# Summing the exponentials of two groups on VectorE before the product with ones, in unit 3 of an attention layer

## What is computed

```python
attn = jnp.einsum('bhqd,bhkd->bhqk', Q, K) * scale
attn = jnp.where(causal, attn, -jnp.inf)
probs = jax.nn.softmax(attn, axis=-1)
y = jnp.einsum('bhqk,bhkd->bhqd', probs, V)
y = y.transpose(0, 2, 1, 3).reshape(Bx, Sx, Dm)
return y @ W_O.T
```

## Time and profile before

| | us |
|---|---|
| median of 3 runs | 2440.8 (2438.86 to 2441.42) |
| profiled execution | 2442.9 |
| its span, first to last instruction | 2441.2 |
| PE busy | 2295.5 (94%) |
| DVE busy | 1453.3 (60%) |
| ACT busy | 1072.6 (44%) |
| POOL busy | 861.4 (35%) |
| product with ones (den_ps), 3072 instructions | 319.0 |
| product with v (y_ps), 3072 instructions | 327.3 |

### The profile page before, as it was taken

One profiled execution on the slowest core, in us unless ns is written; L12 is line 12 of the kernel. 1 busy time (PEld: TensorE's weight loads), 2 busy tenths in 40 slices (PEclk: granted clock), 3 DMA queues, 4 the chain that ended last, 5 costly groups with the idle time before them and its releaser, 6 DMA issues.

```text
span 2441.2 us, 42231 instructions
## 1 busy us (share of the span) xinstructions
PE 2295.5 (94%) x14012; PEld 1467.3 (60%) x14013; DVE 1453.3 (60%) x3928; ACT 1072.6 (44%) x2186; POOL 861.4 (35%) x1519
## 2 busy tenths in 40 slices
PE   1999999999999999999999999999999999959998
PEld 1755575547654675457554765477546755437886
DVE  2577366644775367736674576537763667466776
ACT  2245424462345324542446234632454244625665
POOL 2232324232423333332423242334233242235666
PEclk9999999999999999999999999999999999969999
DMA  8533145313533154314432353225322444344554
GB/s 297 148 96 104 61 113 150 111 66 91 152 102 103 45 159 109 97 64 120 147 105 70 87 158 102 96 55 172 103 80 70 128 119 122 102 148 134 162 163 130
DMA packets 131537, 283.11 MB, mean 116 GB/s; under 512 B 33110, under 2 KB 42334, under 8 KB 128928
## 3 DMA queue, kind: packets, MB, share of 16 engines
q1 hardware_dynamic: 102352, 212.79, 29.3%
q0 software_dynamic: 27472, 67.49, 9.5%
q10 hardware_dynamic: 1536, 0.53, 0.1%
HBM read 135.10 MB, written 46.48 MB: 74 GB/s over the span
## 4 chain that ended last, share of the span: by engine, by line
PE 78%; DVE 7%; SPq 5%; DMA 3%; ACT 2%; issue 2%; POOL 1%; ACTq 0%; POOLq 0%; DVEq 0%
PE y_ps L1349 12%; PE proj L1260 10%; PE den_ps L1349 10%; PE score L1329 10%; PE maxp L1317 8%; PE proj L1372 5%; SPq L514 5%; PE proj L1273 4%; PE maxp L1514 4%; PE score L1514 4%; PE proj L1317 3%; PE maxp L1329 2%; DVE tile_max L1008 2%; PE score L1372 2%; ACT probs L872 2%
## 5 line engine op out<-in xcount | busy, mean ns | idle before, releaser
L872 ACT ACTIVATE probs<-score 128x512 f32<-128x512 f32 (+3 forms) x1216 | 563.5, 493 | 541.5 <-PE score L1329 519.8
L712 POOL TENSOR_SCALAR_AFFINE_SELECT probs<-probs 128x256 f32<-128x256 f32 x512 | 217.0, 428 | 707.1 <-ACT probs L872 704.2
L1013 DVE CUSTOM_DVE_ANT_0 maxp<-maxp,mask_qk 128x384 f32<-128x384 f32 (+3 forms) x696 | 323.1, 505 | 215.2 <-PE maxp L1317 209.4
L1329 PE MATMUL score<-q_stack,k_stack 97*128 97x512 f32 (+2 forms) x1216 | 425.9, 373 | 23.5 <-ACT probs L872 21.4
L1260 PE MATMUL proj<-xt,w_qk 128*128 128x512 f32 x1284 | 363.3, 399 | 54.3 <-DMA w_qk<-w_qk_parts 53.4
L1317 PE MATMUL maxp<-k_stack,q_stack 96*128 96x512 f32 (+2 forms) x1024 | 329.3, 365 | 11.4 <-DVE tile_max L1008 4.4
L1349 PE MATMUL y_ps<-probs,v 128*32 128x512 f32 (+3 forms) x3072 | 327.3, 498 | 12.1 <-DVE rows L1038 12.0
L1349 PE MATMUL den_ps<-probs,ones_f 128*32 128x512 f32 (+3 forms) x3072 | 319.0, 486 | 0.0
L1329 PEld LDWEIGHTS score<-q_stack,k_stack 97*128 97x128 f32 x1216 | 224.4, 189 | 139.5 <-ACT probs L872 92.3
L1260 PEld LDWEIGHTS proj<-xt,w_qk 128*128 128x128 f32 x1284 | 237.9, 190 | 110.3 <-DMA w_qk<-w_qk_parts 51.2
L1317 PEld LDWEIGHTS maxp<-k_stack,q_stack 96*128 96x128 f32 x1024 | 180.3, 188 | 137.3 <-DVE tile_max L1013 44.6
(11 more groups left out here) (159 smaller groups left out, 3157.2 us busy)
## 6 DMA issues: line engine op xcount, KB each, us to landing
w_qk<-w_qk_parts SPq DMA_DIRECT2D x64, 512.0 KB, 4.1
q_stack<-w_vo_parts SPq DMA_DIRECT2D x16, 2048.0 KB, 8.1
q_stack<-parts SPq DMA_DIRECT2D x512, 64.0 KB
k_stack<-parts SPq DMA_DIRECT2D x512, 64.0 KB
rows<-dispatched SPq DMA_DIRECT2D x75, 257.0 KB, 2.9
xt_raw<-x_t SPq DMA_DIRECT2D x32, 512.0 KB, 3.8
q_stack<-parts POOLq DMA_DIRECT2D x256, 64.0 KB, 2.3
k_stack<-parts POOLq DMA_DIRECT2D x256, 64.0 KB, 2.3
```

The source lines that it names most:

```text
L712: nc.gpsimd.affine_select(out=block, in_=block, compare_op=ALU.is_ge, fill=0.0, base=0, pattern=[[0, 2], [1, P]], channel_multiplier=-1)\
L872: nc.scalar.activation(probs[:, 4 * (n % PROBS) + h, c:BANK], score_bank(u, 4 * j + h)[:, c:BANK], ACT.Exp, scale=SCALE).then_inc(exp_done ...
L1013: top = nc.vector.tensor_tensor_reduce(out=tile, in0=tile, in1=mask_qk[:, BANK - cols:BANK], scale=1.0, scalar=-3.0e38, op0=ALU.add, op1=A ...
L1329: nc.tensor.matmul(score_bank(u, i)[:, c0:BANK], k_st[u % SETS][0:3 * DH + 1, h, kb * P:(kb + 1) * P], q_st[u % SETS][0:3 * DH + 1, h, t * ...
```

## The change

In unit 3 of every pass, groups 4 and 5, and groups 6 and 7, form a pair (`PAIRS`). VectorE adds the two groups' exponentials, all four heads in one instruction of 128 x 4 x 512, into a new tensor `late_sum` (`add_pair`). The product with ones is left out for the first group of a pair, and for the second it reads `late_sum`. So there are two groups of products with ones where there were four. The product with v stays for each group, and now signals `probs_used` for these. ScalarE waits for the pair's sum before it overwrites one of its groups (groups 7 to 10). The first add stands in VectorE's order at group 6 between `copy_y` and `turn_sums`, the second at group 8 ahead of the first residual. There is one `late_sum`, so the second add also waits for the first pair's product.

`late_sum` lies in the same memory as `w_qk`. The loads of unit 0's weights are therefore moved from `send(b, 3)` to behind `load_x(2)`, with a wait for the second pair's product.

```diff
--- before.py
+++ after.py
@@ -181,6 +181,8 @@
         with nc.sbuf_tensor("last_weight", [P, 2 * KT * D], F32), nc.sbuf_tensor("bias", [P, EXPERTS * D], F32) as bias:
             pass
         probs = sb("probs", [P, 4 * PROBS, BANK])
+        with nc.sbuf_tensor("late_sum", [P, 4, BANK], F32) as late_sum:
+            pass
         w_qk = sb("w_qk", [P, 2, 2, KT, P], F32R)
         parts = sb("parts", [P, 2, 2, BANK], F32R)
         rows = sb("rows", [P, ROWT, ROW])
@@ -289,6 +291,9 @@
         exp_done = signal("exp_done", UNITS * STILES)
         probs_masked = signal("probs_masked", UNITS * 2 * DIAGONAL)
         probs_used = signal("probs_used", UNITS * GROUPS)
+        PAIRS = ((4, 5), (6, 7))
+        pair_added = signal("pair_added", len(PAIRS))
+        pair_used = signal("pair_used", len(PAIRS))
         y_copied = signal("y_copied", UNITS * HALVES)
         sums_copied = signal("sums_copied", UNITS * HALVES)
         recip_done = signal("recip_done", UNITS * HALVES * 2)
@@ -498,6 +503,12 @@
             t, kb = SCORE_GROUPS[j]
             return kb * P >= t * BANK
 
+        assert all(SCORE_GROUPS[j][0] == 1 and SCORE_GROUPS[j][1] < HALF0 for pair in PAIRS for j in pair)
+
+        def pair_of(u, j):
+
+            return next((p for p, pair in enumerate(PAIRS) if u == UNITS - 1 and j in pair), None)
+
         def masks_up_to(u, j):
 
             return 2 * (DIAGONAL * u + sum(map(diagonal, range(j + 1))))
@@ -534,8 +545,8 @@
                 for o in (Q, K):
                     for t in range(HALVES):
                         send_tile(sp, b, u, o, t, range(SP_BLOCKS), sp_in)
-                    if not (u == UNITS - 1 and b == BATCHES - 1):
-                        load_w((u + 1) % UNITS, o)
+                    if u < UNITS - 1:
+                        load_w(u + 1, o)
 
             def load_expert(e):
                 if e >= RAWS:
@@ -591,6 +602,10 @@
                 for tb in range(2, ROWT):
                     wait_job(sp, b, proj_free, ("o", tb - 2))
                     load_x(tb)
+                    if tb == 2 and not last:
+                        sp.wait_ge(pair_used.sem, pair_used.at(b, len(PAIRS)))
+                        load_w(0, Q)
+                        load_w(0, K)
                 if not last:
                     send(b, 0)
 
@@ -866,6 +881,9 @@
                             split_high(k, xt_in[k % 2].at(b, 16 * (k // 2 + 1)))
                         n = GROUPS * u + j
                         weighed(act, b, max(n - PROBS + 1, 0))
+                        over = pair_of(u, j - PROBS)
+                        if over is not None:
+                            act.wait_ge(pair_added.sem, pair_added.at(b, over + 1))
                         for h in range(4):
                             c = column(kb, t)
                             act.wait_ge(score_full.sem, score_full.at(b, 4 * n + h + 1))
@@ -1038,6 +1056,14 @@
                     nc.vector.tensor_copy(y_of(n), y_ps[:, :].rearrange("p (t q) -> p t q", q=P))\
                         .then_inc(y_copied.sem, 1)
 
+                def add_pair(u, p):
+
+                    first, second = [probs[:, 4 * ((GROUPS * u + j) % PROBS):4 * ((GROUPS * u + j) % PROBS) + 4, :]
+                                     for j in PAIRS[p]]
+                    scored(dve, b, GROUPS * u + PAIRS[p][1] + 1)
+                    dve.wait_ge(pair_used.sem, pair_used.at(b, p))
+                    nc.vector.tensor_tensor(late_sum[:, :, :], first, second, ALU.add).then_inc(pair_added.sem, 1)
+
                 squares = lambda a: a.rearrange("p (c r) -> p c r", r=DH)
 
                 def turn_sums(n):
@@ -1095,9 +1121,13 @@
                             turn_sums(2 * u - 1)
                         if j == HALF0 + LAG:
                             copy_y(2 * u)
+                            if u == UNITS - 1:
+                                add_pair(u, 0)
                             turn_sums(2 * u)
                             if u == UNITS - 1:
                                 divide(2 * u)
+                        if u == UNITS - 1 and j == PAIRS[1][1] + 1:
+                            add_pair(u, 1)
                         due = maxima(u, j)
                         for i in due[0:2]:
                             reduce_tile(u + 1, i)
@@ -1341,16 +1371,25 @@
                         pe.wait_ge(exp_done.sem, exp_done.at(b, 4 * (n + 1)))
                         if diagonal(j):
                             pe.wait_ge(probs_masked.sem, probs_masked.at(b, masks_up_to(u, j)))
-                    if kb == 0:
+                    pair = pair_of(u, j)
+                    if sums_too and pair is not None:
+                        if j == PAIRS[pair][0]:
+                            return
+                        pe.wait_ge(pair_added.sem, pair_added.at(b, pair + 1))
+                    first = (j if pair is None or not sums_too else PAIRS[pair][0]) in (0, HALF0)
+                    if first:
                         free = sums_copied if sums_too else y_copied
                         pe.wait_ge(free.sem, free.at(b, half))
                     for h in range(4):
                         head = 4 * u + h
                         mm = nc.tensor.matmul((den_ps if sums_too else y_ps)[DH * h:DH * (h + 1), c:BANK],
                                               ones_f[:, :] if sums_too else v[:, kb, head * DH:(head + 1) * DH],
-                                              probs[:, 4 * (n % PROBS) + h, c:BANK], start=kb == 0, stop=last,
+                                              late_sum[:, h, :] if sums_too and pair is not None else
+                                              probs[:, 4 * (n % PROBS) + h, c:BANK], start=first, stop=last,
                                               tile_position=(0, DH * h), skip_group_check=True)
-                    if sums_too:
+                    if sums_too and pair is not None:
+                        mm.then_inc(pair_used.sem, 1)
+                    elif sums_too or pair is not None:
                         mm.then_inc(probs_used.sem, 1)
 
                 def transpose_max(u):
```

## The result

The changed kernel takes 2458.7 us (median of 4 runs, 2456.2 to 2462.2) where the kernel before took 2440.6 beside it: 1.0071 times as long, 95% interval 1.0056 to 1.0087. That is 18.1 us slower. The forecast was 2455.6.

What follows compares the result with a forecast made beforehand. TensorE, busy in 94% of the span, was taken to bound the kernel. Eight passes each 1.0 longer (-1.72 + 0.4 + 2.3) gave +8.0, the clock +6.8: 2440.8 + 14.8 = 2455.6 us, range 2443 to 2465.

Steps and rivals of the forecast that it cites:

- The gain: Unit 3, TensorE: two groups of sums removed at 0.86 each, 1.72 a pass, at most 13.8 us in eight passes.
- The first pair: Groups 4 and 5: TensorE stands 0.4 for the turned sums, and the product ends 0.46 earlier than before.
- The second pair: Groups 6 and 7: the add holds GpSimd's low part, TensorE stands 2.3 before output 0, pass 1.0 longer.
- The bound from the masks: GpSimd masks stood until VectorE's two-input instruction ended; so y's low part ends 1.15 behind the add, +1.0 a pass.
- rival B: The low part isn't held by the add; output 0 starts 0.55 earlier each pass, 2436.4 us; chance 0.13.
- The last pass: VectorE's splitting of expert weights stands between the adds; taken as the other passes, bounds 0 to +2.3.
- the add is always first: Unit 3: the second add starts ahead of GpSimd's low part, which also needs ScalarE's high part.
- The clock: TensorE's 2.3 us stall can bring 3.4 us at half speed, about 1.7; taken in four passes, +6.8, bounds 0 to +13.6.
- rival A: The forecast itself: low part held, clock falls in two to seven passes, 2452.2 to 2460.7 us; chance 0.42.
- A2: Low part held, clock falls in at most one pass: 2448.8 to 2450.5 us, down to 2443.2; chance 0.27.
- The sum: Whole kernel: +8.0 for the passes and +6.8 for the clock make +14.8, so 2455.6 us.
- The moved loads: Unit 0's weight loads in SyncE's queue: cost nothing, with over 20 us of cover; without it up to 6 us a pass.

Runs made afterwards that it cites:

- e8_early_high: Changed kernel with the order of e6_both, plus ScalarE making y tile 0's high part in the middle of group 7; 0.9937 of the kernel before, -15.4 us.
- e6_both: Changed kernel with the second add waiting for the low parts of y tiles 0 and 1, and the turning ahead of the first add; 0.9973 of the kernel before.
- e1_low_first: Changed kernel with VectorE's second add waiting until GpSimd has made the low parts of y tiles 0 and 1; 0.9986 of the kernel before, -3.4 us.
- e5_split: Changed kernel with the second add cut into four instructions of 128x512, one a head; 0.9986 of the kernel before, -3.4 us.
- e3_second_pair: Changed kernel with only groups 6 and 7 added on VectorE, groups 4 and 5 keeping their own products; 1.0103 of the kernel before, +25.2 us.
- e10_fill9: Changed kernel with nine throwaway matmuls on TensorE ahead of output 0's wait; 1.0027 of the kernel before, +6.6 us.
- e4_moved_loads: Changed kernel with no pairs or adds, only unit 0's weight loads moved; 0.9998 of the kernel before, -0.5 us.

## Why the prediction was right

**The gain** was taken as 2 x 0.86 = 1.72 a pass. e8_early_high, where nothing else arrives late in seven of the passes, gives 1.86 a pass there, 13.6 us in all eight unit 3s, and 15.4 us in all against the 13.8 that I took as the most; within its interval (11.0 to 19.6) that is the same.

**The first pair.** Forecast: a wait of about 0.4 for the turned sums, and the product done 0.46 earlier than before. Measured: the wait is 0.41 in seven passes (2.9 us in all), but the product behind it took 1.07 where 0.86 was put, so it was done 0.25 earlier. The eight instructions themselves are hardly slower. TensorE's timeline of before has, in the row from which the 0.86 was read:

```profile
531.21 1.07 PE L1349 MATMUL y_ps<-probs,v 128*32 128x512 f32 x8
532.09 1.04 PE L1349 MATMUL den_ps<-probs,ones_f 128*32 128x512 f32 x8
```

From first start to last end they took 1.04 there too, but the first 0.19 of it lay under the end of the product with v (532.28), and behind a wait that overlap is gone. Alone the pair gives 0.26 a pass. The step was right and the term 0.2 too good. e6_both removes the wait, and unit 3 is 0.62 a pass shorter than in e1_low_first, which is the 0.41 and the 0.21 together.

**The second pair.** The order was as forecast: group 7's exponentials, at once the add, and the low part inside it. From the end of the add to that of the low part I had 1.15, and it was 1.13; e1_low_first and e5_split, with the same work, show that the place of the add and the length of one instruction decide. The bound from the masks thus held for a subtraction with two operands too, as the Trainium skill ("SBUF — State Buffer", Who interferes with whom) has it, and rival B is out. Output 0 started 1.27 later than before in place of 1.0; the 0.2 of the first pair's product is most of the difference.

**The last pass** I had between 0 and +2.3, taken as +1.0. Its timeline:

```profile
2133.13 2.28 DVE L992 TENSOR_TENSOR weight<-w_raw,weight 128x2048 fp32r<-128x2048 f32 x1
...
2134.97 4.66 POOL L734 TENSOR_TENSOR parts<-rows,parts 128x512 fp32r<-128x512 f32 x2 [11.79 <-ACT parts L861]
...
2135.33 3.35 DVE L1065 TENSOR_TENSOR late_sum<-probs 128x2048 f32<-128x2048 f32 x1
...
2136.68 3.01 PE L1411 MATMUL proj<-q_stack,parts 128*128 128x512 f32 x12 [1.07 <-POOL parts L734]
```

Here the low part came while the expert's subtraction ran, ended 1.12 behind it at 2136.53, and VectorE's add, which was queued, stood until then: 3.35 in place of 2.29. GpSimd got in first, TensorE stood 1.07, and the pass lost 0.3 at most. So "the add is always first" was wrong for this pass, in which VectorE comes to the add only behind the expert's subtraction, and so was the fear that the add would slip in ahead of a low part that already waits; e5_split shows the latter in every pass.

**The clock.** Each stall of 2.36 could cost 1.7, in four of eight passes as I took it, from one row of before. It costs 1.6 (4.57 against 2.94), and it came in seven passes of one profile and four of the other, and in six of eight of e3_second_pair: 17 of 22 such stalls, where I had taken half. The four passes were a choice between none and eight and not worked out from anything, so this term was too small, and nothing in the rows of before could have sized it. So rival A stands, with the profile of the first result at its upper end, and A2 (no falls) is what e10_fill9 shows when the falls are taken away, +6.6 (4.1 to 9.3) to be compared with the forecast of +8; of the changed kernel itself no profile was without falls.

**The sum.** From the profile: seven passes with 1.27 + 1.6 and a last with 0.3 are 20.4 us in unit 3 (7 x 2.86 + 0.2 by the exponentials); the spans differ by 16.6 and the medians by 18.1. The rest, some 2 to 4 us the other way, lies in unit 0 and in the closing and opening between passes. The latter are 2.8 shorter in all than before, but in the variants, all of which have the same loads moved, they are anything from 2.6 shorter to 3.4 longer, so nothing follows from it for the change. My sum of 14.8 was put together from 8.0 of hold (measured 9.2) and 6.8 of clock (11.2 in one profile, less in the other). Both terms were too small, by 5.6 together, and that the forecast of 2455.6 came within 3.1 us of the measured 2458.7 is in part luck, since 2 to 4 us went the other way elsewhere. The mechanism is what the prediction had right.

**The moved loads** were put at nothing, and e4_moved_loads says the same.

## What to carry to other kernels

Before work is moved to an idle VectorE, look at what GpSimd does in the same microseconds, and at who waits for GpSimd: the second add, of two SBUF tensors, had slack itself (TensorE never waited for its sum) and yet held a subtraction of 1.29 us until it was over. When such an add has slack, let it wait for the urgent GpSimd instruction, or cut it into pieces; both turned 18 us slower into 3 faster. Where a stall of TensorE can't be avoided, price the clock as well: here it was about half of the loss (10.5 of 17.1 us by the times with and without the fill, 11.2 of 20.4 in unit 3 of the first profile).

## What the runs showed of the hardware

- In every overlap looked at here, an instruction on VectorE with two SBUF inputs and a subtraction or mask on GpSimd, which read SBUF, excluded each other, both ways: the low part took 2.86 behind an add, an add 3.35 and a quarter of one 1.78 behind a low part. The later one ended about as long behind the earlier as its own work, less some 0.15. Beside a VectorE instruction with one SBUF input (0.70) the low part took 1.28, as alone.
- Between two such instructions queued on VectorE a waiting GpSimd instruction got its turn, in the last pass and in every pass of e5_split.
- A stall of TensorE of 2.36 us, in otherwise dense work, was followed by 3.4 us at half clock in seven of seven cases of one execution, in four of seven of another and in six of eight of e3_second_pair (two of these 17 falls lasted 6.8 us); stalls of 0.8 and of 1.1 us were followed by none in unit 3. (In six of the ten later profiles one or two falls came at other places in a pass, so stalls of this kind are not the only occasion.) With matmuls that did nothing useful in the stall there was no fall in a unit 3.
- A group's product that starts behind a wait took 1.07 on the chain where it takes 0.86 in a row of others, whose first 0.19 overlapped the product ahead.
